# A fused graph, expert and attention kernel: the first three pairs of expert weights loaded in the graph stage, and the first normalization split between VectorE and ScalarE

## What is computed

```
def reference(x, src, dst, edge_weight, ...):
    x = x + graph_conv_0(layernorm(x), edges, ...)      # low-rank product, then two GCN layers of 256 and 768
    x = x + switch_moe(layernorm(x), ...)               # 16 experts, at most 64 tokens each, 768 -> 384 -> 768
    x = x + graph_attention_1(layernorm(x), edges, ...) # two GAT layers
    x = x + expert_attention(layernorm(x), ...)         # three attention experts, gated
    return x
```

## Time and profile before

| | |
|---|---|
| runs | 1711.87, 1712.66, 1713.43 us; median 1712.66 |
| the profiled execution's own time | 1712.41 us |
| its span, first to last instruction | 1711.2 us |
| busy | TensorE 1432.6 us (84%), VectorE 1016.9 (59%), ScalarE 551.6 (32%), GpSimd 208.0 (12%) |
| moved by DMA | 102.47 MB |

### The profile page before, as it was taken

The page is one execution under the profiler, slowest core; times in us unless marked ns, Lnnn a source line. Parts: engine busy times, 40 slices in busy tenths (PEclk is TensorE's granted clock), DMA queues, the critical chain, the costliest instruction groups (busy, mean ns, idle before and its releaser), DMA issues. The chain is left out here.

```text
span 1711.2 us, 24706 instructions
## 1 busy us (share of the span) xinstructions
PE 1432.6 (84%) x8462; PEld 1107.7 (65%) x8463; DVE 1016.9 (59%) x1869; ACT 551.6 (32%) x1271; POOL 208.0 (12%) x324
## 2 busy tenths in 40 slices
PE   4898988999287479718888869999889999999997
PEld 3577776856143245417787845555568898898987
DVE  7588886267411459989999945612236452363254
ACT  2588880004310251115555531300022231231122
POOL 0122220400020000000000022000046103102100
PEclk8899998999589669959999989999989999999999
DMA  5000001021899713101212021000021001000011
GB/s 154 1 0 0 0 0 47 1 83 29 311 324 392 240 47 86 46 1 30 60 31 60 1 80 30 1 0 0 0 67 47 19 1 47 29 1 28 10 46 46
DMA packets 78374, 102.47 MB, mean 60 GB/s; under 512 B 33898, under 2 KB 58599, under 8 KB 77167
## 3 DMA queue, kind: packets, MB, share of 16 engines
q1 hardware_dynamic: 76242, 93.14, 18.0%
q0 software_dynamic: 1280, 6.29, 1.0%
q10 hardware_dynamic: 770, 1.92, 0.4%
HBM read 90.33 MB, written 11.01 MB: 59 GB/s over the span
## 5 line engine op out<-in xcount | busy, mean ns | idle before, releaser
L1517 PE MATMUL ps<-B,gat_room 125*125 125x97 f32 x1600 | 196.3, 279 | 76.1 <-DVE gat_room L1477 76.1
L1517 PEld LDWEIGHTS ps<-B,gat_room 125*125 125x125 f32 x1600 | 183.7, 191 | 89.1 <-DVE gat_room L1477 86.7
L513 PE MATMUL ps<-gat_room,g_A 125*128 125x250 bf16 x1600 | 182.7, 272 | 21.7 <-ACT g_A L547 21.7
L513 PEld LDWEIGHTS ps<-gat_room,g_A 125*128 125x128 bf16 x1600 | 153.0, 98 | 46.1 <-ACT g_A L547 29.7
L1270 DVE CUSTOM_DVE_ANT_0 g_junk<-g_srow,MN 125x1250 bf16<-125x1250 f32 x90 | 138.7, 1541 | 21.5 <-DMA g_srow<-ald 15.0
L547 ACT ACTIVATE g_A<-g_A,g_act_edges 125x128 bf16<-125x128 bf16 x400 | 127.7, 390 | 41.2 <-DVE g_A L472 41.2
L1472 ACT ACTIVATE gat_room<-gat_room,g_scol 125x1250 f32<-125x1250 f32 x80 | 106.9, 1338 | 103.7 <-DVE gat_room L1466 103.7
L1466 DVE SCALAR_TENSOR_TENSOR gat_room<-g_ab,g_scol 125x1250 f32<-125x1250 f32 x80 | 120.4, 1506 | 2.8 <-PE ps L1517 2.3
L1477 DVE SCALAR_TENSOR_TENSOR gat_room<-gat_room,CT 125x1250 f32<-125x1250 f32 x80 | 116.1, 1451 | 1.3 <-ACT gat_room L1472 1.3
L1459 PE MATMUL ps<-gat_room,A 128*125 128x384 f32 x240 | 80.2, 498 | 0.0
L1459 PE MATMUL ps<-gat_room,B 128*125 128x384 f32 x240 | 79.4, 495 | 0.0
(11 more groups left out here) (364 smaller groups left out, 2860.5 us busy)
## 6 DMA issues: line engine op xcount, KB each, us to landing
expert_w<-in_L_ffn_wi_dram SPq DMA_DIRECT2D x10, 1152.0 KB, 12.2
g_ab<-abd SPq DMA_DIRECT2D x9, 1093.8 KB
arena<-in_L_ffn_wo_dram SPq DMA_DIRECT2D x8, 1152.0 KB, 14.5
gat_room<-in_L_ffn_wi_dram SPq DMA_DIRECT2D x6, 1152.0 KB, 16.2
expert_w<-in_L_ffn_wo_dram SPq DMA_DIRECT2D x6, 1152.0 KB, 13.8
g_srow<-ald SPq DMA_DIRECT2D x9, 546.9 KB
c_fold_w<-in_L_gnn_W_dram SPq DMA_DIRECT2D x12, 384.0 KB, 5.1
gat_room<-in_L_gnn_W_dram SPq DMA_DIRECT2D x4, 1152.0 KB, 12.1
```

What stands on the lines that cost most here:

```text
L513: last = nc.tensor.matmul(sums[:, off:off + T * WIN], A[:, h, i, g, :], G[:, h, g, :], start=False, stop=True, skip_group_check=True)
L1517: last = nc.tensor.matmul(ps[:NT, bank, at:at + C + 1], P[:, i % PR, t * NT:(t + 1) * NT], hx[:, s, h, :], start=(s == 0 and t % GO == 0), ...
```

## The change

Four things are edited.

The four buffers of the expert ring are made at the start of the program (`expert_w0`, `expert_w1`, and two areas in `arena` and the room of the attention weights). Until their weights come, the first two serve as room for small tables of the graph stage, cut out by a new helper `carve`; `fold_w`, `prod` and `tmp` of `gcn` move into `XT`'s area.

`gcn` loads pair 0 at its head, pair 1 after part 3 of the first fold, and pair 2 after the last product `aggT`. Since `fold_w` now lies in `XT`, its loads wait until all ten node products are done. `route` loads pair 3 alone, stores the rows, and loads the small bias `b1` last.

In the first normalization ScalarE normalizes tiles 3, 4, 7, 8 and 9 itself (bias and scale per row), between its copies; VectorE computes the bias (`shift`) for five tiles at a time.

TensorE turns the marks ahead of tiles 8 and 9, not after them.

```diff
@@ norm_and_turn
+        by_act = (3, 4, 7, 8, 9) if shift is not None else ()
+        by_dve = [t for t in range(T) if t not in by_act]
...
-                for t in range(T)[parts[i]]:
+                if shift is not None:
+                    nc.vector.scalar_tensor_tensor(shift[:, parts[i]], stat[:, parts[i], 0], -1.0, stat[:, parts[i], 2],
+                                                   ALU.mult, ALU.mult).then_inc(shift_done, 1)
+                for t in [t for t in by_dve if t // (T // 2) == i]:
                     nc.vector.tensor_scalar(dst[:, t, :], src[:, t, :], stat[:, t, 0:1], stat[:, t, 2:3],
                                             ALU.subtract, ALU.mult).then_inc(normed, 1)
...
+            def norm_act(t):
+                act.wait_ge(shift_done, t // 5 + 1)
+                nc.scalar.activation(dst[:, t, :], src[:, t, :], ACT.Identity, bias=shift[:, t:t + 1], scale=stat[:, t, 2:3]).then_inc(normed_act, 1)
+
+            def copy(g):
                 act.wait_ge(turned, g + 1)
                 tensor, bank = place(g, out)
                 nc.scalar.activation(tensor, bank, ACT.Copy).then_inc(hi_out, 1)
+
+            deviations(0)
+            if shift is None:
+                deviations(1)
+            for i, t in enumerate(by_act):
+                if i == 2:
+                    deviations(1)
+                norm_act(t)
+                copy(2 * i)
+                copy(2 * i + 1)
+            for g in range(2 * len(by_act), len(groups)):
+                copy(g)
...
                 if h == 0:
-                    pe.wait_ge(normed, t + 1)
+                    if t == T - 2 and "tensor" in beside:
+                        beside["tensor"](pe)
+                    if t in by_act:
+                        pe.wait_ge(normed_act, by_act.index(t) + 1)
+                    else:
+                        pe.wait_ge(normed, by_dve.index(t) + 1)
...
-            if "tensor" in beside:
-                beside["tensor"](pe)
@@ carve
+def carve(nc, c, slot, prefix):
+    taken = [0]
+    def sb(name, shape, dt=F32):
+        words = -(-math.prod(shape[1:]) * (2 if dt in (BF16, I16) else 4) // 32) * 8
+        if taken[0] + words > slot.shape[1]:
+            return c.enter_context(nc.sbuf_tensor(prefix + name, shape, dt))
+        flat = slot[:shape[0], taken[0]:taken[0] + words]
+        taken[0] += words
...
+    return sb
@@ gcn
-        fold_w, prod = sb("fold_w", [128, FR, D]), sb("prod", [128, 2, D])
...
+        f0 = T * H
+        fold_w = room[:, f0:f0 + FR * D].rearrange("p (i n) -> p i n", i=FR)
...
         def _(sp):
+            load_pair(sp, ins, ring, 0)
+            sp.wait_ge(hw_done, T)
             for layer in range(2):
...
                     sp.dma_start(fold_w[:, j % FR, :], ins[f"L1_gnn_W{layer + 1}"].rearrange("(k p) n -> p k n", p=128)[:, k, :]).then_inc(fold_in[j % FR], 16)
+                    if j == FR:
+                        load_pair(sp, ins, ring, 1)
...
                 sp.dma_start(moe["lnw"][p0:p1], ins["L0_ffn_ln_w"].partition_broadcast(p1 - p0)).then_inc(moe["lnw_in"], 16)
+            sp.wait_ge(aggT_done, 6)
+            load_pair(sp, ins, ring, 2)
@@ route
-            for j in range(SLOTS):
-                load_pair(sp, ins, ring, j)
-            sp.dma_start(g["b1"][:], ...
+            load_pair(sp, ins, ring, 3)
             for t in range(0, T, 2):
                 sp.wait_ge(scaled, t + 2)
                 for p0, p1 in ROWS:
                     sp.dma_start(normd[0:N, :]..., XN[p0:p1, t:t + 2, :]).then_inc(stored, 16)
+            sp.dma_start(g["b1"][:], ...
@@ program
+                slots = [early.enter_context(nc.sbuf_tensor(f"expert_w{i}", [128, 2 * K * FF], F32)) for i in range(2)]
+                ring = expert_ring(nc, early, slots + [arena[:, T * D:T * D + 2 * K * FF], g["room"][:, 0:2 * K * FF]])
...
-                                      banks=(5, 6, 7))
+                                      banks=(5, 6, 7), shift=moe["xb"])
```

More of the change, by code:

```diff
@@ L383, in dense_graph @@
         act_edges = sb("act_edges", [EPC, GR])
-        A = sb("A", [EPC, 2, 4, HALF_GR, 128], BF16)
+        A = tab["A"]
         G = low["spare"][:EPC, 0:GR * T * WIN // 2].bitcast(BF16).rearrange("p (r g n) -> p r g n", r=2, g=HALF_GR)
@@ L568, in _, with gcn @@
             copy_out(NWIN - 1, 6)
-def gcn(nc, ins, low, XT, MT, X, W, stat, ones, ps, g, early, XN, eps_col, moe):
+def gcn(nc, ins, low, XT, MT, X, W, stat, ones, ps, g, early, XN, eps_col, moe, ring):
     H = H_GCN
@@ L800, in expert_ring @@
 def expert_ring(nc, c, rooms):
-    own = c.enter_context(nc.sbuf_tensor("expert_w", [128, SLOTS - len(rooms), 2, K * FF], F32))
-    ring = {"w": [own[:, i, :, :] for i in range(SLOTS - len(rooms))] + [r.rearrange("p (i f) -> p i f", i=2) for r in rooms],
+    ring = {"w": [r.rearrange("p (i f) -> p i f", i=2) for r in rooms],
             "in": [new_sem(nc, c, f"expert_in{i}") for i in range(SLOTS)]}
@@ L2332, in program @@
                 with ExitStack() as dense:
-                    low = graph_inputs(nc, dense, g["room"])
+                    low = graph_inputs(nc, dense, g["room"], slots[1])
                     tables = ExitStack()
-                    tab = edge_tables(nc, tables, low)
+                    tab = edge_tables(nc, tables, low, slots[0])
                     with ExitStack() as s:
```

38 lines of the change are left out of this document (20 added, 18 removed).

## The result

The changed kernel took a median of 1696.72 us in four runs (1694.76 to 1699.87), the kernel before 1713.05 us beside it; the ratio is 0.9905 with a 95% interval from 0.9887 to 0.9922. The forecast was 1691.7 us, with a range from 1688 to 1698.5. Two more sets of runs gave 1695.76 us, 0.9913 [0.9893, 0.9933], and 1695.89 us, 0.9899 [0.9873, 0.9926]. So the gain is 16 to 18 us by the medians (15 to 17 by the ratios), where 20.7 was forecast. The profiled execution took 1699.87 us, the slowest of its four, with a span of 1698.7 us.

A forecast was written before the change was run, and what follows sets the result against it. Bound: the gather waits for row stores queued behind 9.4 MB of expert weights. Routing 18.7, moved pairs 0 and first stage 2.0 us sum to 20.7; 1712.4 less that gives 1691.7 us, range 1688 to 1698.5.

The forecast's parts named there:

- The routing stage: Three of four weight pairs leave `route`, so stores land earlier and the gather starts at 452.85, not 471.55: 18.7 us gained.
- no effect: Rival: something other than the stores holds the gather to 471.55; only 2.0 us gained, 1710.4 us; chance 0.01.
- the other 5.34 MB at 381 GB/s: Routing: after the queue's start-up, pair 3 and stores take 14.0 us more, so the last bytes pass at 450.0.
- the gather starts 2.85 us after the last bytes: Routing, trace of before: last bytes at about 468.7, gather at 471.55; the 2.85 us were added again for 452.85.
- Late stores: Rival: stores move at the x loads' rate, or the last land later behind pair 3; 1696.6 us, chance 0.13.
- wrong if the gather came 4 us or more after the token list: Routing: stated sign of being wrong; the forecast had the gather at 452.85 after the token list at 451.57.
- The pairs that moved: Graph stage: loading pairs 0, 1 and 2 there was claimed to cost nothing, 0 us; up to 7.5 us at worst.
- that leaves 2 us: First fold: pair 1 lands at 362.3, load 4 1.0 us later, 2 us before VectorE wants it at 365.55.
- The first stage: Normalization shared with ScalarE: stage ends 0.9 us earlier, low-rank product gains 1.1; 2.0 us together, bounds -1 and 3.2.
- I take 1.1, half: Low-rank product: at most 2.3 us to gain if TensorE enters it at 2.4 GHz; half of that taken.
- Warm experts: Rival: with a shorter pause before the gather TensorE keeps 2.4 GHz, shortening the first expert's product; 1689.4 us, chance 0.06.
- slower: Rival: load 4 of the first fold lands 20.7 us late behind pair 1, time above 1712 us; chance 0.02.

The follow-up runs named there:

- the doubled pair: Changed kernel with pair 0 loaded not at the head of `gcn` but together with pair 1, between fourth and fifth load of the first fold; 1694.79 us.
- the first stage's part: Kernel before with only the new first normalization (ScalarE's share, marks turned earlier, `shift`); run twice: 1712.74 us (0.9992) and 1712.99 us (0.9999).

## Why the prediction was right, and where its sum was off

The direction, the mechanism and the range held. Step by step, with the means of the table's executions with and without the part in question:

**The routing stage** (18.7 us forecast). From the loop to the load back 179.55 us became 161.63 (four executions against seven): 17.9 us. The stores are what the gather waited for, and "no effect" is out: the gather starts 1.6 us behind their last bytes in all of these eleven. Two terms of the sum were mis-sized and partly cancel. The step "the other 5.34 MB at 381 GB/s" puts the last bytes 53.4 us after the start of the loop (450.0 less 396.57); they passed 55.8 us after it in the trace of after, 56.2 in the mean of the seven, as the stores fell to 292 GB/s at their end. The step "the gather starts 2.85 us after the last bytes" was read from a stretch of 4 us as if its bytes had passed at full rate; it is 1.6. So the gather is gained by 17.4 us, and the experts behind it took 0.5 us less (103.83 against 104.32 from the gather to the load back). "Late stores" has a part, the last stores landing late; the rate of the x loads, 257 GB/s, would have cost 4.9 us. The sign "wrong if the gather came 4 us or more after the token list" hit in five of the seven profiles (3.0 to 6.2 us): the queue, and not the token list, is still the limit. Of the other signs, the stores came from 430.5 to 443.3, as forecast, and TensorE's wait was 10.02 us where 7 was forecast.

**The pairs that moved** (0 forecast). No DMA wait inside the first fold of the profile of after. But the step "that leaves 2 us" fell: the slack is some 0.2 us, as the doubled pair showed, and two executions had a wait, 0.31 and 0.64 us, which the prediction named as a sign of being wrong. The step took the 6.5 us of the earlier trace rows as the time of both loads. It is the median of the two, and the second took 7.8 us; pair 1's second load took 8.9, and load 4 came 1.0 us behind it, as the step had it. From the first biased node product to the loop it is 134.54 us with the moved weights (nine, without the doubled pair) and 132.99 without (four): 1.5 us are lost here. Most of it, 1.3 us, is at the first load of the second fold (waits of 7.9 us in the mean against 6.6), and 0.5 at the normalization weights (4.1 against 3.6), with small terms the other way. Pair 1 is through by the second fold; why this load takes longer wasn't tried and stays open. So does the wait for the normalization weights, behind which pair 2 goes out.

**The first stage** (0.9 + 1.1 us forecast, bounds -1 and 3.2). The product starts 1.6 us earlier (42.32 in ten executions, 43.89 in four), and the first biased node product follows it 2.3 us sooner (215.82 against 218.15): 3.9 us, above the upper bound. The step "I take 1.1, half" was the mis-sized one: in six of ten executions the product ran all at the upper level (granted clock 1.00), 5.22 us. Part of it is the execution's, as a product of 6.78 us without the first stage's part shows.

**The sum.** 17.9 - 1.5 + 3.9 is 20.3 us, near the forecast 20.7 by errors that cancel; that part of the agreement is luck. The three profiles of after are 19 to 24 us ahead at the second attention layer, 21.7 in the mean, their rest is 1.4 us longer (719.2 against 717.8 in the two of before), and the times of just these executions are 20.3 us apart. All timed runs, most of them without a profile, are only 16 to 18 us apart. Where the others lose the difference can't be read. The silent step of the sum, that the rest of the program, untouched, takes what it took, is the one that the profiles put in doubt: it was made on one profile of before, which has the shortest rest but two of the fourteen, and in the first profile of after the rest was 7.0 us longer. The falls of the clock go with the length of the rest in the fourteen profiles. Whether an earlier start brings more of them, or fourteen profiles happened to fall so, stays open: the leads of the first stage's part, 6.6 and 3.9 us of which 1 us is left in the time, speak for the former; the rests, spread over 9 us in the changed kernel alone, leave room for the latter.

"Warm experts" did not come (the first product of the experts took 5.98 us, and 6.14 before), and "slower" was far away.

## What to carry to other kernels

A queue that carries both what is wanted next and what is wanted later should carry the first first: with the stores ahead of the weights, the gather followed the token list by 1.1 us. Don't carry a rate or a landing time from one stretch to another as a fixed price: the same stores moved at 413 GB/s behind the weights of the kernel before, and at 292 and at 280 to 306 elsewhere, and a median of two loads hid that the second took 7.8 us. A mean over 4 us can't place the last byte within 1 us. And before a few microseconds of a sum are believed or missed, profile the same kernel two or three times and compare stage by stage: stages that the change doesn't touch differed by up to 9 us between executions. The stage in question repeated within 1.4 us in four profiles with the old order, and within 2.4 in six of the seven with the new one, the seventh lying 2.8 above these.

## What the runs showed of the hardware

TensorE's granted clock falls in the middle of dense work: 0.60 in a stretch of 4 us with TensorE busy for all of it, while the same stretch of another execution of the same program shows 1.00. This one fall stands 289 or 290 us after the second attention layer's weights in ten of the fourteen profiles, and TensorE had no gap over 0.1 us in the 5 us ahead of it in any of them. The other falls, 49 in all from 268 us after these weights to TensorE's last product, stand behind a pause: in the 5 us ahead of each, TensorE was idle for 1.8 to 3.6 us. One of them, of the kernel before (the pause, then the stretch with it and the one behind it; clock third from the end):

```profile
1344.81 0.40 PE L2005 MATMUL ps<-ident,a_outs 125*128 125x125 f32 x2 [2.19 <-issue]
```

```profile
1341.00:1345.80 4.80, 2.60 (x18) 2.07 (x17) 3.53 (x10) 1.45 (x6) 4.64 (x4) 1.00 0.21 62
1345.88:1349.20 3.32, 3.31 (x12) 3.03 (x11) 1.73 (x6) 0.30 (x2) 0.20 (x1) 0.50 0.47 139
```

The Trainium skill, page "TensorE: Matmul & The Clock Gate", section "Part 1: The HAM clock gate", says that the monitor behind this clock runs freely and doesn't start with the kernel, so that a program meets it at another point each time; the low-rank product of 5.22 us in six executions and up to 7.59 us in others fits that. The section speaks of an idle engine ahead of a fall. Most falls here agree, and the one at 1264 us shows one without that; its cause stays open.

The end of a block with ten stores has a steady price: 1.61 to 1.63 us from the last bytes of the stores to the gather behind them, in twelve executions.
